# A decoder layer: self attention's queries and keys projected in tiles of 128 tokens that cross batch borders

## The reference, cut to what matters

```python
x = _rmsnorm(tokens, norm_w)
q = x @ Wq
k, v = jnp.split(x @ Wkv, 2, axis=-1)
q = _head_rmsnorm(split(q), q_gamma)   # q / max(|q|, 1e-12) * (gamma + 1) * 8, per head
k = _head_rmsnorm(split(k), k_gamma)
sim = jnp.tanh(einsum('bhid,bhjd->bhij', q, k) / 50) * 50 * 64 ** -0.5
out = einsum('bhij,bhjd->bhid', softmax(sim), v) @ Wo      # heads side by side
x = _layernorm(x + out)
```

## Time and profile before

| | us |
|---|---|
| median of 3 runs | 1805.52 |
| lowest and highest | 1804.0, 1807.37 |
| the profiled execution, its own time | 1807.37 |
| its span in the profile | 1805.3 |

### The profile page before, as it was taken

The page is one execution under the profiler, slowest core; times in us unless marked ns, Lnnn a source line. Parts: engine busy times, 40 slices in busy tenths (PEclk is TensorE's granted clock), DMA queues, the critical chain, the costliest instruction groups (busy, mean ns, idle before and its releaser), DMA issues.

```text
span 1805.3 us, 37470 instructions
## 1 busy us (share of the span) xinstructions
PE 1753.1 (97%) x13957; PEld 1478.4 (82%) x13957; DVE 1403.3 (78%) x3229; ACT 1184.9 (66%) x2691; POOL 1109.1 (61%) x1250
## 2 busy tenths in 40 slices
PE   8999999999998899999999999999999999988997
PEld 7777777778877899999999999899899899974443
DVE  6777778787888677777777788777777777787887
ACT  6878887756755566666666667666556666665775
POOL 3434445664566586786686655677787778551454
PEclk9999999999998999999999999999999999999999
DMA  5223323111105422432432523314313332534553
GB/s 206 76 67 98 98 77 109 47 32 46 48 22 173 137 90 99 152 100 78 153 109 68 174 90 85 112 49 125 96 50 112 96 95 71 125 92 106 124 134 97
DMA packets 141106, 176.80 MB, mean 98 GB/s; under 512 B 63884, under 2 KB 99088, under 8 KB 140928
## 3 DMA queue, kind: packets, MB, share of 16 engines
q1 hardware_dynamic: 122392, 138.15, 25.3%
q0 software_dynamic: 14656, 28.92, 5.9%
q10 hardware_dynamic: 3880, 7.35, 1.4%
...
## 4 chain that ended last, share of the span: by engine, by line
PE 78%; DVE 7%; DMA 5%; ACT 5%; POOL 4%; issue 2%; ACTq 0%; POOLq 0%; DVEq 0%
PE att_ps_T L552 7%; PE att_ps_SA L1755 5%; PE att_ps_P L1731 5%; PE att_ps_P L1719 4%; PE att_ps_SB L612 4%; PE att_ps_P L552 4%; PE att_ps_P L1783 4%; PE att_ps_T L1719 4%; PE att_ps_O L1719 3%; PE att_ps_SB L600 3%; PE att_ps_T L1731 3%; PE att_ps_P L1769 3%; PE att_ps_O L1731 3%; PE att_ps_P L1794 2%; DMA ca_ct<-ct_kept 2%; POOL sa_p_lo L423 2%
## 5 line engine op out<-in xcount | busy, mean ns | idle before, releaser
L1537 POOL TENSOR_TENSOR ca_pr<-ca_pr,ca_rec 112x750 f32<-112x750 f32 x256 | 366.5, 1452 | 189.6 <-DVE ca_rec L2017 186.7
L423 POOL TENSOR_TENSOR sa_p_lo<-sa_pr,sa_p_hi 112x448 fp32r<-112x448 f32 x128 | 146.6, 1159 | 210.9 <-ACT sa_p_hi L718 210.0
L1902 ACT ACTIVATE ca_big<-att_ps_P 126x384 fp32r<-126x384 f32 (+1 forms) x254 | 105.3, 449 | 66.5 <-PE att_ps_P L1769 65.1
L1896 ACT ACTIVATE ca_pr<-att_ps_SA,ca_nmax 112x750 f32<-112x750 f32 x128 | 113.6, 887 | 22.0 <-DVE ca_nmax L2013 11.2
L887 DVE RECIPROCAL sa_sums<-sa_sums 128x224 f32<-128x224 f32 x64 | 99.1, 1548 | 34.1 <-ACT sa_sums L727 33.8
L2022 DVE TENSOR_TENSOR ca_big<-att_ps_P,ca_big 126x384 fp32r<-126x384 f32 (+1 forms) x254 | 119.7, 498 | 6.2 <-ACT ca_big L1902 5.9
L2013 DVE TENSOR_REDUCE ca_nmax<-att_ps_SA 112x1 f32<-112x752 f32 x128 | 119.1, 930 | 1.2 <-PE att_ps_SA L1755 1.1
L2013 DVE TENSOR_REDUCE ca_nmax<-att_ps_SB 112x1 f32<-112x752 f32 x128 | 119.0, 930 | 0.0
L1731 PE MATMUL att_ps_P<-ca_w_hi,ca_ct 128*126 128x256 f32 x558 | 114.2, 284 | 1.4 <-DVE ca_q_lo L1996 1.4
L1896 ACT ACTIVATE ca_pr<-att_ps_SB,ca_nmax 112x750 f32<-112x750 f32 x128 | 113.1, 883 | 0.1
L1769 PEld LDWEIGHTS att_ps_P<-att_ident,ca_pr 64*126 64x126 f32 (+1 forms) x1524 | 86.0, 138 | 15.2 <-issue 10.8
...
## 6 DMA issues: line engine op xcount, KB each, us to landing
...
```

What stands on the lines that cost most here:

```text
L423: pool.tensor_tensor(p_lo[:, h % NB, :], pr[:, h % NB, :], f32(p_hi[:, h % NB, :]), ALU.subtract).then_inc(p_split, 1)
L1537: pool.tensor_tensor(w, w, rec[:, h % PB, c:c + 1].to_broadcast([R, S]), ALU.mult).then_inc(norm_done, 1)
L1896: act.activation(pr[:, h % PB, c, :].rearrange("r (a s) -> r a s", a=2), two_halves(psum[slot]), ACT.Exp, bias=nmax[:, h % PB, c:c + 1], a ...
L1902: act.activation(weights_view(h, c, x, False), blocks_view(source.bank, x), ACT.Copy).then_inc(t_hi_done, 1)
```

## The change

**Tiles.** Tokens are numbered through the batches, and queries and keys are projected in tiles of P = 128 tokens. Four batches have 7 tiles, so the batches project 2, 2, 2 and 1 tiles (`TILES_OF`), and the fourth of each four, batches 3 and 7, one. For a tile over a border the transposed x of the next batch must be there: x is loaded and transposed three batches ahead of the attention instead of two (`AHEAD`), and `xt`, `q` and `k` are rings of columns (`XW`, `RING_PIECES`, `TILE_COLUMNS`). V stays in chunks of 112 tokens. Projections and transposes of q and k load 128 columns.

**Orders.** Where the batch projected has one tile (steps 2, 6, 10 and 14) TensorE, ScalarE and VectorE have an order of their own (`WITH_ONE_TILE`; Q1 and K1, still named in it, do nothing), and V0 takes the bank of Q1. In `UNITS` the transposes of x stand last, so that their banks, P0 and P1, are those of K0 and Q1; Q1 waits until x of the next batch is transposed.

**Copies.** For batches 1 and 5 the parts of q and k are copied in two pieces each, for batches 2 and 6 an additional copy of 64 columns of x is made (`wraps`). `th` and `sq` have two buffers instead of four.

**The guard.** The guard of the head norms is needed per row of a tile, not of a chunk. `ss` goes to a tile-wise copy by three or four small transfers on SyncE's queue (`spread_squares`) for the first eight batches, and `guards` (U) computes the guard once for each of them, ahead of N1; L838 is gone.

**Start.** x[1] is loaded into `y` right behind x[0] and ahead of the weights. Its squares and transposes come ahead of Q0's squares.

```diff
@@ self_attention @@
-    AHEAD = 2
+    AHEAD = 3
+    PERIOD = 4
+    XW = 2 * N + HALF
+    TILE_COLUMNS = [[0, P], [2 * P, 3 * P], [HALF, HALF + P], [2 * P + HALF]]
+    TILES_OF = [[0, 1], [2, 3], [4, 5], [6]]
+    RING_PIECES = [[(0, 0, 2 * P)], [(0, 2 * P, P + HALF), (P + HALF, 0, HALF)], [(0, HALF, 2 * P)], [(0, 2 * P + HALF, P)]]
-    UNITS = """XT0 XT1 Q0 K0 Q1 K1 V0 T0 V1 T1 T2 T3""".split()
-    units = [(u, f"P{i % 3}") for i, u in enumerate(UNITS)]
+    UNITS = """Q0 K0 Q1 K1 V0 T0 V1 T1 T2 T3 XT0 XT1""".split()
+    units = [(u, f"P{(i + 2) % 3}") for i, u in enumerate(UNITS)]
@@ sync @@
+        def spread_squares(m):
+            if m:
+                sp.wait_ge(ss_spread, spread_count(m - 1))
+            for c, r, n, t, row in pieces_of(m):
+                sp.dma_start(tile_ss[row:row + n, t:t + 1], ss[r:r + n, m % 2, c:c + 1]).then_inc(ss_spread, 16)
...
         load_rows(x[0], None)
+        sp.dma_start(y[:, :, :], x[1].rearrange("(c r) n -> r c n", r=R)).then_inc(x_in_second, 16)
         load_weights(0, range(2))
@@ tensor, project @@
+            if u[0] != "V" and c >= len(tiles(at)):
+                return
+            if u == "Q1":
+                for t in range(2):
+                    pe.wait_ge(drained[slot[f"XT{t}"]], drained_count(f"XT{t}", lambda per, k: at(per, k) + per))
...
-                mm = pe.matmul(ps(u)[0:R, :], xs[:, k, c * R:c * R + R], ws[i][:, k, :],
+                mm = pe.matmul(ps(u, at)[0:rows, :], xs[:, k, col:col + rows], ws[i][:, k, :],
@@ tensor, orders @@
-        ORDERS = [steps("""S1 O0 O1 S2 Q0+ O2 O3 K0+ S3 O4 O5 Q1+ O6 O7 K1+ V0+ Y0 T0+ V1+ T1+ S0+ T2+ Y1 T3+ X++"""),
+        ORDERS = [steps("""S1 O0 O1 S2 Q0+ O2 O3 K0+ S3 O4 O5 Q1+ O6 O7 K1+ V0+ Y0 T0+ V1+ T1+ S0+ T2+ Y1 T3+ X+++"""),
...
+        WITH_ONE_TILE = steps("""S1 O0 O1 S2 Q0+ O2 O3 S3 K0+ Q1+ K1+ O4 O5 V0+ O6 O7 V1+ Y0 T0+ T1+ S0+ T2+ Y1 T3+ X+++""")
@@ scalar @@
-        NEXT_SPLITS = {"K1": (4, range(KC)), "W2": (5, range(3)), "T0": (5, range(3, KC))}
+        NEXT_SPLITS = {"V0": (4, range(KC)), "W2": (5, range(3)), "T0": (5, range(3, KC))}
@@ vector @@
         def mean_squares(at):
             dve.wait_ge(ss_done, at(2, 2))
-            dve.tensor_scalar(guard[:, :], ss[:, :], 1e-24 / DM, 1e-24 * RMS_EPS, ALU.mult, ALU.add).then_inc(rows_done, 1)
-            dve.tensor_scalar(ssq[:, 0, ROWS], ss[:, :], 1.0 / DM, RMS_EPS, ALU.mult, ALU.add).then_inc(rows_done, 1)
+            dve.tensor_scalar(ssq[0:R, 0, ROWS], ss[:, number(at) % 2, :], 1.0 / DM, RMS_EPS, ALU.mult, ALU.add).then_inc(rows_done, 1)
```

More of the change, by code:

```diff
@@ L231, in pair_view, with place, slot_of, counts_for @@
         return bass.AP(t, v.offset, [v.ap[0], (VP, NP), (2 * D, 2), (1, D)])
-    def ps(u):
-        return bank[slot[u]]
+    def place(u, at):
+        if len(tiles(at)) == 1 and u in ("Q1", "V0"):
+            return {"Q1": "V0", "V0": "Q1"}[u]
+        return u
+    def slot_of(u, at):
+        return slot[place(u, at)]
+    def counts_for(u, at):
+        absent = {"Q0": "K1", "K0": "Q1"}.get(u)
+        if absent is None or len(tiles(at)) == 2:
+            return 1
+        assert slot_of(absent, at) == slot[u] and uses_before(absent, at) == uses_before(u, at) + 1
+        return 2
+    def ps(u, at=None):
+        return bank[slot[u] if at is None else slot_of(u, at)]
+    def one_tile(batches):
+        return batches[1] is not None and len(tiles(batches[1][1])) == 1
     filled = {s: sem(f"filled_{s}") for s in bank}
@@ L311, in step_before, with pieces_of, spread_count @@
         return at(plan.uses[slot[u]], 1)
-    def sync(sp):
+    def pieces_of(m):
+        pieces = []
+        for c in range(2):
+            token, end = m * N + c * R, m * N + c * R + R
+            while token < end:
+                n = min(end, token // P * P + P) - token
+                pieces.append((c, token - m * N - c * R, n, token // P, token % P))
+                token += n
+        return pieces
+    def spread_count(m):
+        return 16 * sum(len(pieces_of(n)) for n in range(m + 1))
+    def sync(sp):
+        def spread_squares(m):
[3 more added lines that the diff above has]
+                sp.dma_start(tile_ss[row:row + n, t:t + 1], ss[r:r + n, m % 2, c:c + 1]).then_inc(ss_spread, 16)
         def load_weights(g, which):
@@ L593, in values @@
             if h == 0:
[L594 to L595 removed]
+                for s in ("V0", "V1"):
+                    pe.wait_ge(drained[slot_of(s, at)], drained_count(s, at))
             pe.wait_ge(p_split, at(HG, h + 1))
@@ L637, in step @@
             batches = batches_of(b, g)
-            for name, n in ORDERS[g]:
+            for name, n in WITH_ONE_TILE if one_tile(batches) else ORDERS[g]:
                 if batches[n]:
@@ L1001, in step @@
             batches = batches_of(b, g)
-            for name, n in ORDERS[g]:
+            for name, n in WITH_ONE_TILE[g] if one_tile(batches) else ORDERS[g]:
+                if name == "U" and g * B + b == -AHEAD + 1:
+                    continue
+                if name == "N0.0" and g * B + b == -1:
+                    guards(counter(0, 0, B))
                 if batches[n] and not (isinstance(b, int) and g * B + b + n == GROUPS * B - 1 and name[0] in "ID") and not (
```

283 lines of the change are left out of this document (188 added, 95 removed).

## The result

The changed kernel is slower. Its runs took 1811.12, 1813.72, 1817.12 and 1821.02 us (one disturbed run is left out), a median of 1815.42; over the kernel before, 1804.0 us median in five runs, the ratio is 1.0049 with the 95% interval [1.0028, 1.0070]. The profiled execution took 1821.02 us and is the slowest of these four; its span is 1819.2 us, 13.9 us more than before, where the ratio says 9 us.

The account below looks back on a forecast made before the run. TensorE's own work was taken as the bound in self attention. Terms from -13.5 us (three one-tile steps) to +4.3 (start) summed to -6.05, giving 1799.5 us against the median of 1805.52; the range was 1790.0 to 1807.5.

Parts of the forecast that it names:

- What bounds the kernel, what is removed: Self attention: TensorE's own work is the bound; 6.4 us a step removed in four steps, 25.6 us gross.
- the +3.45 foreseen: Steps 1, 3, 4, 5, 8, 9, 11, 12: narrower ScalarE and VectorE changes and the guard add 3.45 us.
- Three of the four steps: Steps 2, 6, 10: waits of 1.2 us at S0 and 0.6 in Y0 leave 4.5 us gained a step, -13.5.
- The splits in step 6: Step 6: group 1's weight splits stand ahead of T0 on ScalarE and TensorE waits, +2.3 us.
- the narrower changes: ScalarE and VectorE: split copies +1.2, extra copy +0.65, wider copies +0.5; also wider transposes +0.5 us.
- The fourth step and the handover: Step 14 into cross attention: load of x at most 1.9 us sooner, half taken, -0.9; x's transposes gone, -0.5.
- The start: Ahead of batch 0: loading x[1] before the weights and its squares and copies cost +4.3 us, 3 to 5.
- The +1.8 of the last step ahead of batch 0: Start, ScalarE's chain: two squares of x, an extra copy and wider T copies add 1.8 us.
- The +2.5 ahead of it: Start: K0 near 16.2 us instead of 13.71, behind squares and copies, the x[1] load (1.15 us) included.
- Step 7: Step after the splits: the 1.20 us wait for the low part of x goes, -1.2 us.
- Widened loads: 672 projections load 128 columns instead of 112: hidden, 0 us; rival that they are paid, 1810, chance 0.03.
- The clock: Rival: idle one-tile steps lower TensorE's clock, 6.8 us a fall, slower from the second (1813; 1826 with four), chance 0.05.

Follow-up runs that it names:

- with the waits filled: Changed kernel with idle products put into TensorE's waits in self attention (start and one-tile steps): 1815.51 us, 1.0041 of the kernel before.
- The experiments with the store: Scaling of y moved earlier on GpSimd in step 14: in the changed kernel 1808.8 us, 1.0022; in the kernel before 1802.71 us, 0.9987.
- the rearranged kernel without idle products: Changed kernel with start, VectorE's order in one-tile steps and store of y rearranged, no idle products: 1801.6 us, 0.9976 of the kernel before.

## Why the prediction was wrong

It gave 1799.5 us, and 1790.0 to 1807.5; the measured ratio puts the kernel 9 us above the one before. Three terms failed most. In the profile the clock, which the sum put at nothing, is 8.6 of the 17.9 us between forecast and trace, the start 3.2 and the handover 3.1 without it. In the order of its steps:

**What bounds the kernel, what is removed.** Right. TensorE's work shrank as counted: step 2 is 3.94 us shorter and has 2.43 us of waits, together 6.37 against 6.4. Six of the eight normal steps are 0.2 to 0.9 us longer and two are not; that their sum is the +3.45 foreseen is partly luck, since no run tested its terms one by one.

**Three of the four steps.** The mechanism was right, both waits are there and S0's has its size (1.08 against 1.2). Y0's was mis-sized: 1.35 instead of 0.6 us. The step put the chain behind O7 at its length before, and allowed for less work on VectorE; but I2, D2 and Q0's and K0's scalings now stand in a row ahead of I3, and they hold the chain up (0.74 us with K0's behind I3). The splits in step 6 were put too high: 2.3 us, where S0's wait grew from 1.08 to 1.75 and the step, with the waits filled, is 1.1 us longer than step 2 (31.28 against 30.14). Step 10 has the same two waits as step 2 (1.40 and 1.08 us) and is only 2.97 us shorter than before; steps 8, 9 and 12 are 0.8 to 0.9 us longer too. That points to the narrower changes and is not shown.

**The fourth step and the handover.** That the handover goes by SyncE's queue was right, and its size was wrong: -1.4 foreseen with x's transposes, +1.7 found, and +2.2 behind it, which is the clock's. The step took from the load of x half of the 1.9 us by which V1 lets it go sooner, and held the store to its place. But GpSimd came to the scaling of y only behind the fourth pair's parts, 23.6 us into the step, and the store at 25.65 instead of 24.2, 1.4 us later. The load of x, though issued 0.5 us earlier in the step, then took 9.3 us from issue to use instead of 7.4, because it stands closer behind the store and the context's loads; first product and store are 11.7 us apart as before. The experiments with the store show 5 to 7 us in the changed kernel and 2.3, hardly clear of noise, in the one before.

**The start.** +4.3 foreseen, with 5 as the upper end; +7.5 found with the waits filled. The +1.8 of the last step ahead of batch 0 held: in that kernel step 0, where S2 waits for its tanh, is 1.8 us longer. The +2.5 ahead of it is what failed, since T0 is 5.5 us late. The load of x[1] cost 2.1 us and not 1.15: ScalarE waited 1.92 us for Wq. The squares and the copies that K0 waits for were counted, but they start 2.3 us later than the squares did before (12.50), and K0 is 3.7 us late instead of 2.5:

```profile
14.77 0.61 ACT L806 ACTIVATE sa_x_sq<-sa_y 112x512 f32<-112x512 f32 x1
...
16.00 0.94 ACT L874 ACTIVATE sa_xt_hi<-att_ps_P 128x512 fp32r<-128x512 f32 x2
```

And the guard, for which the prediction had 0.6 us in all of its eight places, took 1.29 us at the start alone, with 0.51 of waiting behind it, on the chain to T0:

```profile
29.72 1.29 DVE L982 TENSOR_SCALAR sa_guard<-sa_tile_ss 128x2 f32<-128x2 f32 x1
31.53 0.24 DVE L1006 TENSOR_SCALAR att_ps_O<-att_ps_O,sa_guard 128x16 f32<-128x16 f32 x1 [0.51 <-DVE sa_guard L982]
```

**Step 7.** The wait that was to go (1.2 us) went, and O6 waited 2.20 us for the low part of p in its place, behind GpSimd's and VectorE's weight blocks (GpSimd stood idle for 1.75 us ahead of it until VectorE had the pair's output). With the waits filled, and in the rearranged kernel without idle products, it is 0.6 us or absent, and which order of events brings it was not isolated. That stays open.

**Widened loads.** Zero was right but for about 1 us. A projection of 12 products with 128 columns loaded and, behind it, V0's with 112, from the chain of waits:

```profile
100.25 2.81 PE att_ps_T L660 x12
103.06 2.79 PE att_ps_P L660 x12
```

2.81 and 2.79 us, 234 and 233 ns a product, where 112 columns gave 232 before. Over 56 projections 0.02 us each would be 1.1 us, an estimate from these two rows. The Trainium skill ("TensorE: Matmul & The Clock Gate", section "LDWEIGHTS (loading the stationary operand)") puts a load at its columns / 1.2 ns; 16 columns more, paid in full, would by that have made about 245 ns of the 232, an estimate from the page. The 234 measured show that the load is hidden.

**The clock.** The sum put it at nothing, and this rival, slower from the second fall on, had 0.05. It came in part: five stretches in self attention where there had been none, and 10 us more at the handover. Where it was wrong is the argument against it, that one wait of 1.2 us had not lowered the clock: here pairs of waits of that size sometimes did and sometimes didn't. And its price was too high: a fall lasts 3.41 us mostly and costs 1.5 us, not 6.8, and the 23.9 us at the handover cost 2.2. Of the 17.9 us between forecast and trace, 8.6 are the clock's in that profile (6.4 in self attention, by the filled kernel, and 2.2 at the handover); in the timed runs its share was not resolved. The other 9.3 us are the start (3.2), steps 13 to 15 (3.1), the one-tile steps (1.5) and step 7 (1.4), each taken too small, and 0.15 of the normal steps.
